# A recurrent GRU and RK4 kernel on one core: GRU work moved on VectorE, ScalarE and GpSimd, and four short matmuls a stage

## The reference

```python
# block 0: GRU, state h
gi = x @ W_ih + b_ih;  gh = h @ W_hh + b_hh
r = sigmoid(i_r + h_r);  z = sigmoid(i_z + h_z)
n = tanh(i_n + r * h_n)
h_new = (1 - z) * n + z * h
# block 1: four Runge-Kutta stages a time step, state q, p; drive = x + GRU's output at this step
i_couple = tanh(q) @ coupling.T
dq = q - q**3 / 3 - p + drive + i_couple + bias
dp = EPSILON * (q + ALPHA - BETA * p)
```

## Time and profile before

| what | us |
|---|---|
| median of 3 runs (lowest, highest) | 3659.93 (3659.13, 3660.63) |
| the profiled execution | 3661.45 |
| its span, first to last instruction | 3659.7 |
| TensorE matmul busy (share) | 3546.2 (97%) |
| TensorE weight load busy | 3220.4 (88%) |
| VectorE busy | 2998.4 (82%) |
| ScalarE busy | 2574.2 (70%) |
| GpSimd busy | 1507.0 (41%) |
| mean granted TensorE clock | 0.989 |

### The profile page before, as it was taken

One profiled execution on the slowest core, in us unless ns is written; L12 is line 12 of the kernel. 1 busy time (PEld: TensorE's weight loads), 2 busy tenths in 40 slices (PEclk: granted clock), 3 DMA queues, 4 the chain that ended last, 5 costly groups with the idle time before them and its releaser, 6 DMA issues.

```text
span 3659.7 us, 298613 instructions
## 1 busy us (share of the span) xinstructions
PE 3546.2 (97%) x115469; PEld 3220.4 (88%) x115469; DVE 2998.4 (82%) x20699; ACT 2574.2 (70%) x22689; POOL 1507.0 (41%) x6169
## 2 busy tenths in 40 slices
PE   8989999999999999999999999999999999999978
PEld 4479999999999999999999999999999999999954
DVE  2078888888888888888888888888888888888876
ACT  3257777777777777777777777777777777777753
POOL 0034444444444444444444444444444444444421
PEclk9999999999999999999999999999999999999978
DMA  3000000000000000000000000000000000000001
GB/s 127 23 25 1 1 1 1 1 1 1 1 1 1 1 1 1 1 1 1 1 1 1 1 1 1 1 1 1 1 1 1 1 1 1 1 1 1 1 2 46
DMA packets 9454, 24.45 MB, mean 7 GB/s; under 512 B 557, under 2 KB 601, under 8 KB 8793
## 3 DMA queue, kind: packets, MB, share of 16 engines
q1 hardware_dynamic: 8832, 19.92, 1.5%
q10 hardware_dynamic: 88, 0.02, 0.0%
HBM read 15.75 MB, written 4.19 MB: 5 GB/s over the span
## 4 chain that ended last, share of the span: by engine, by line
PE 79%; DVE 14%; issue 4%; ACT 3%; DVEq 0%; DMA 0%; ACTq 0%; POOL 0%; POOLq 0%
PE psum L1180 43%; PE psum L1138 29%; PE psum L1108 5%; DVE psum L887 2%; DVE tpart L843 2%; DVE gates L776 2%; ACT tpart L571 1%; PE psum L1283 1%; DVE psum L878 1%; DVE psum L866 1%; DVE fresh L795 1%; DVE narg L787 1%; DVE hs L812 1%; ACT tfull L573 1%; DVE hpart L819 0%
## 5 line engine op out<-in xcount | busy, mean ns | idle before, releaser
L1180 PE MATMUL psum<-tpart,cpl 128*128 128x32 f16 x65536 | 1995.8, 177 | 34.1 <-DVE tpart L843 15.0
L1180 PEld LDWEIGHTS psum<-tpart,cpl 128*128 128x128 f16 x65536 | 1788.7, 96 | 150.9 <-DVE tpart L843 41.5
L1138 PE MATMUL psum<-hpart,whh 128*128 128x32 f16 x49152 | 1622.9, 176 | 28.8 <-DVE hpart L819 24.4
L1138 PEld LDWEIGHTS psum<-hpart,whh 128*128 128x128 f16 x49152 | 1404.1, 96 | 91.5 <-DVE hpart L819 30.4
L843 DVE SCALAR_TENSOR_TENSOR tpart<-tfull,tpart 128x8 f16<-128x8 f32 x4096 | 668.4, 163 | 146.6 <-ACT tfull L573 9.9
L571 ACT ACTIVATE tpart<-psum 128x8 f16<-128x8 f32 x3072 | 544.0, 177 | 245.8 <-DVE psum L887 177.2
L887 DVE TENSOR_REDUCE psum<-psum 128x8 f32<-128x24 f32 x3072 | 585.5, 192 | 133.9 <-PE psum L1180 12.2
L573 ACT ACTIVATE tfull<-psum 128x8 f32<-128x8 f32 x3072 | 529.2, 172 | 0.0
L571 ACT ACTIVATE tpart<-qnext 128x8 f16<-128x8 f32 x1024 | 213.9, 209 | 434.6 <-DVE qnext L887 434.5
L535 ACT ACTIVATE qterm<-psum 128x16 f32<-128x16 f32 x3072 | 400.6, 184 | 111.0 <-DVE psum L866 109.1
L374 POOL TENSOR_TENSOR kept<-rz,hs 128x8 f32<-128x8 f32 x1024 | 209.2, 204 | 466.5 <-ACT rz L500 465.6
(11 more groups left out here) (152 smaller groups left out, 4040.5 us busy)
## 6 DMA issues: line engine op xcount, KB each, us to landing
xrow<-in_x_dram SPq DMA_DIRECT2D x4, 1024.0 KB, 11.3
out_dram<-space SPq DMA_DIRECT2D x16, 256.0 KB, 2.0
wih<-in_L_cond_W_ih_dram SPq DMA_DIRECT2D x3, 1024.0 KB, 9.6
space<-in_L_cond_W_hh_dram SPq DMA_DIRECT2D x1, 3072.0 KB, 18.6
space<-in_L_cond_coupling_dram SPq DMA_DIRECT2D x1, 1024.0 KB, 19.2
xrow<-in_cond_dram SPq DMA_DIRECT2D x1, 1024.0 KB, 4.7
wih<-in_L_cond_Wk_dram SPq DMA_DIRECT2D x1, 1024.0 KB, 5.6
wih<-in_L_cond_Wo_dram SPq DMA_DIRECT2D x1, 1024.0 KB, 8.0
```

What stands on the lines that cost most here:

```text
L1138: mm = pe.matmul(gate_out[x][:, :, :, c * B:(c + 1) * B], whh[:, w, k, n * P:(n + 1) * P], copies_in(hpart[:, k, :, :]), start=(c == 0 and ...
L1180: mm = pe.matmul(stage_out[a][:, :, :, col:col + B], cpl[:, w, k, n * P:(n + 1) * P], copies_in(tpart[:, s % 2, k, :, :]), start=(col == 0 ...
```

## The change

A new tile `omzs` holds omz scaled by s_h; ScalarE fills it (`scaled_omz`, for half 0 in stage 0 behind stage_terms(0), for half 1 in stage 2 behind the first tanh pair), and `weigh` becomes a tensor_tensor of `omzs` and `cand` that waits for it. `split_tanh` becomes a tensor_tensor without the factor 1.0. candidate(1) moves behind the square of stage 2, keep_part(1) on GpSimd behind the sums of stage 2. On VectorE sum_gates(1) moves behind base(2); in stage 3 cubic(3) comes ahead of weigh(1), base(3) ahead of new_high(1), and h_low(1) ahead of the reduction of half a. On TensorE a stage matmul with n = 1 or 3 and k = 3 moves its 8 columns once (`reps`); by the diff these are two matmuls (w = 0, 1) of each half.

```diff
+        omzs = sb("omzs", [P, HALVES, HC])
+        omzs_ready = sem_ab("omzs_ready")
@@ gpsimd, step
-                    if s == 1 and gru <= T:
+                    if s == 2 and gru <= T:
                         keep_part(1, gru)
@@ scalar
+            k_h = act.alloc_register("act_scale_up")
+            act.reg_load(k_h, scale[0:1, 2:3].bitcast(i32))
+            def scaled_omz(x, v):
+
+                act.wait_ge(omz_ready[x], v)
+                act.activation(omzs[:, x, :], omz[:, x, :], ACT.Copy, scale=k_h).then_inc(omzs_ready[x], 1)
@@ scalar, step
                             candidate(0, gru)
+                        if s == 2 and a == 0 and gru <= T:
+                            scaled_omz(1, gru)
                     if s == 2:
                         stage_terms(2)
-                        if gru <= T:
-                            candidate(1, gru)
                     arg, s_next = (in_halves(qnext[:, :]), 0) if s == 3 else (qt, s + 1)
...
                         stage_terms(0)
+                        if gru <= T:
+                            scaled_omz(0, gru)
...
                             sigmoids(1, gru)
+                    if s == 2 and gru <= T:
+                        candidate(1, gru)
                     if s == 2 and gru < T:
                         gate_input(gru + 1)
@@ vector
-                dve.wait_ge(omz_ready[x], v)
+                dve.wait_ge(omzs_ready[x], v)
                 dve.wait_ge(cand_ready[x], v)
-                dve.scalar_tensor_tensor(fresh[:, x, :], omz[:, x, :], s_h, cand[:, x, :],
-                                         ALU.mult, ALU.mult).then_inc(fresh_ready[x], 1)
+                dve.tensor_tensor(fresh[:, x, :], omzs[:, x, :], cand[:, x, :], ALU.mult).then_inc(fresh_ready[x], 1)
...
-                dve.scalar_tensor_tensor(tpart[:, s % 2, a * HK:(a + 1) * HK, 1, :],
-                                         tfull[:, a * HC:(a + 1) * HC].rearrange("p (k b) -> p k b", b=B), 1.0,
-                                         tpart[:, s % 2, a * HK:(a + 1) * HK, 0, :], ALU.mult, ALU.subtract).then_inc(t_parts[s][a], 1)
+                dve.tensor_tensor(tpart[:, s % 2, a * HK:(a + 1) * HK, 1, :],
+                                  tfull[:, a * HC:(a + 1) * HC].rearrange("p (k b) -> p k b", b=B),
+                                  tpart[:, s % 2, a * HK:(a + 1) * HK, 0, :], ALU.subtract).then_inc(t_parts[s][a], 1)
@@ vector, step
                     new_high(0, gru)
                     new_h_full(0, gru)
+                base(2, now)
+                if gated_step:
                     sum_gates(1, gru)
-                base(2, now)
...
+                cubic(3, now)
                 if gated_step:
                     weigh(1, gru)
-                cubic(3, now)
+                base(3, now)
                 if gated_step:
                     new_high(1, gru)
-                base(3, now)
-                if gated_step:
                     new_h_full(1, gru)
-
-                sum_stage(3, 0, now)
                 if gru < T:
                     h_low(1, gru)
+
+                sum_stage(3, 0, now)
                 sum_stage(3, 1, now)
@@ tensor, stage_products
-                            mm = pe.matmul(stage_out[a][:, :, :, col:col + B], cpl[:, w, k, n * P:(n + 1) * P],
-                                           copies_in(tpart[:, s % 2, k, :, :]), start=(col == 0 and k == 0 and w == 0),
+                            reps = 1 if n % HK == HK - 1 and k == K - 1 else COPIES
+                            mm = pe.matmul(stage_out[a][:, 0:reps, :, col:col + B], cpl[:, w, k, n * P:(n + 1) * P],
+                                           copies_in(tpart[:, s % 2, k, :, :])[:, 0:reps, :], start=(col == 0 and k == 0 and w == 0),
```

More of the change, by code:

```diff
@@ L519, in _ @@
                 sigmoids(1, v)
+                scaled_omz(0, v)
+                scaled_omz(1, v)
                 candidate(0, v)
```

## The result

The changed kernel takes 3703.61 us (median of 4 runs, 3702.61 to 3703.99) against 3660.23 for the one before: ratio 1.0119, 95% interval 1.0101 to 1.0136. It is 43.4 us slower, where 53.6 us faster was forecast, and outside the range.

The account below looks back on a forecast made before the run. Stages were taken as bound by a loop of latencies, not TensorE's pace. Gains 0.01 + 0.03 + 0.02 + 0.045 = 0.105 us a step over 510 steps gave 53.6 us, hence 3606 us, range 3574 to 3640.

Parts of the forecast that it names:

- What bounds the kernel: Each stage is a loop of latencies through TensorE and VectorE; TensorE waits 0.07 to 0.34 us in each.
- Eight columns: Stage matmuls ending a half: end about 8 ns sooner, no gain in pace; stages 0 and 1 gain 0.01 us.
- Rival (2): TensorE's stage matmuls: fewer columns also quicken the pace, 0.165 us a step, 3576 us; chance 0.07.
- weigh: VectorE's weigh as tensor_tensor: holds the engine 0.07 us less each time, bounds 0 and 0.15.
- Stage 2: VectorE's new order in stage 2: the split for stage 3 starts 0.02 to 0.06 us sooner; taken as 0.03.
- the exclusion that the prediction names: VectorE tensor_tensor with both inputs in SBUF and GpSimd reading SBUF exclude each other; would cut stage 2's gain to 0.02.
- Stage 3: VectorE's new order from weigh(1) to the reduction of half a: 0.07 to -0.01 us gained, taken as 0.02.
- TensorE's late start of every second stage 0: TensorE's 0.09 us lateness, from gate matmuls waiting for h_low(1), goes: 0.045 us a step gained.
- The gate block of stage 3: Sign on TensorE: with h_low(1) sooner, the gate block lasts 0.77 us and not 0.91.
- (3): VectorE: weigh is no cheaper, delaying sum_gates(1) and stage 3's reduction; 0.035 us a step longer, 3678 us; chance 0.07.
- (1): Only TensorE's stop goes, stages 0 to 2 at lower ends, stage 3 at -0.01; 0.055 a step, 3632 us; chance 0.17.
- (4): The granted clock falls to the half level, half a takes 45 ns longer; 38 us slower, 3698 us; chance 0.03.

Follow-up runs that it names:

- low_back: Changed kernel with h_low(1) moved back between the two reductions of stage 3; 3596.22 us, ratio 0.9824 to the kernel before.
- four_pairs: best_low_behind with four short matmuls at the end of each half instead of two; 3507.07 us, ratio 0.9582 to the kernel before.
- cols_only: The kernel before with the eight-column matmuls alone; 3651.92 us, ratio 0.9977 to the kernel before.
- weigh_stt: low_back with weigh in its old form, scale read from a tensor; 3656.32 us, ratio 0.9987 to the kernel before.
- reorder_only: Changed kernel with all stage matmuls at 32 columns again; 3708.69 us, ratio 1.0130 to the kernel before.
- late_first_low_back: low_back with the late wait written first in weigh, new_high and h_low; 3571.87 us, ratio 0.9760 to the kernel before.
- before_late_first: The kernel before with only the late wait written first in weigh, new_high and h_low; 3569.31 us, ratio 0.9750.
- best_low_behind: late_first_low_back plus the matmuls' wait first in the stage sums (except half a of stage 0) and sum_gates; 3507.67 us, ratio 0.9586 to the kernel before.
- before_waits: The kernel before's order of work with all of best_low_behind's waits and the eight columns; 3528.55 us, ratio 0.9639 to the kernel before.

## Why the prediction was wrong

The step that failed is the sum of stage 3's chain on VectorE from weigh(1) to the reduction. It took two dependent instructions, new_high(1) and h_low(1), for 0.07 us cheaper each than they are, and so saw a gain in moving h_low(1) ahead of the reduction. By terms, forecast and measured:

- *What bounds the kernel*: right. The stages are loops of latencies: in low_back the reduction of stage 3 starts 0.29 sooner and the stage is 0.22 shorter. TensorE's pace wasn't the bound and columns don't set it (four_pairs).
- *Eight columns*: the term holds. 8 ns for a half's end were worked out and 10 measured, and the columns alone are worth 7.5 us (cols_only), where the term's 0.01 a step is 5. Rival (2) is refuted: the starts stay 25 ns apart.
- *weigh*: right within its bounds. Two times 0.07 were put down, two times 0.06 measured (weigh_stt), and its record is 0.167 long and not 0.227. But the 0.11 between the candidate and weigh, in the earlier trace rows, was put down to the read of the scale. It stayed at 0.10 with the scale gone, and fell to 0.04 when the wait was written first.
- *Stage 2*: 0.03 forecast, 0.039 measured. sum_gates(1) behind base(2) did no harm. GpSimd's sums are out of argument(1)'s way, which lasts 0.23 now and not 0.27. keep_part(1) (1536.81 to 1537.01) overlapped its start at 1536.96 and didn't lengthen it, so this trace doesn't bear out the exclusion that the prediction names, for argument's form of instruction; it was not tried by itself.
- *Stage 3*: here it failed, in the terms "base +0.09, new_high(1) +0.09, new_h_full(1) +0.11, h_low(1) +0.19, the reduction +0.11". Measured from weigh's start are 0.11, 0.16, 0.09, 0.26 and 0.11. new_high(1) and h_low(1) each wait for a result that comes last and is the second wait written, 0.07 each above the sum; base brought 0.02, which new_h_full took back, and weigh started 0.34 after the stage's first matmul, 0.02 beyond its upper bound. The reduction came 1.07 after the first matmul, against 0.83 to 0.91 forecast and 0.90 before, and the stage lost 0.125 where 0.02 and 0.045 were to be gained. The rows gave it away: in the earlier trace rows new_h_full ends at 2006.84 and h_low starts at 2006.95, 0.11 later. I took the 0.03 of other pairs.
- *TensorE's late start of every second stage 0*: it was there, and it went, as said. Before, stage 3 lasted 1.705 in one step and 1.797 in the next (means of 200 steps each); in the changed kernel it lasts 1.879 and 1.873. It couldn't be a gain, since the split itself was later than TensorE had been. The gate block of stage 3 lasted 0.83 and not the 0.77 forecast, since h_low(1) starts 0.96 after the stage's first matmul (1.03 before) and not 0.76.
- *Rivals*: the loss was on VectorE in stage 3. (3) had h_low(1) hold the reduction there, but its condition, a weigh that is no cheaper, didn't come, and its price was 18 us. (1) had stage 3 in it with a loss of 0.01 at most. (4) saw the clock fall, but put it down for the whole loop: the falls cover 26 times 3.4 us and cost some 2 us, and with 32 columns throughout (reorder_only) the kernel is as slow with a full clock. Each of the 26 begins in the step behind one of 6.72 to 6.82 us, that is, behind a pause. The changed kernel has 104 steps over 6.7 us and the one before 18. reorder_only has 113 and no fall, cols_only 12 and one, weigh_stt 31 and one; of the kernels faster than these, only low_back has any, 7, and no fall. So the falls of the changed kernel came where its eight columns and its longer steps met; why the clock falls there is open.

## What to carry to other kernels

Before an instruction is put ahead of one on the critical path, take the distance from its producer's end to its start from that very pair in the trace, not from another pair; a dependent chain ahead of the bound instruction costs its idle time besides its busy time (here 0.10 us of waiting ahead of h_low(1)). Where an instruction waits for several semaphores, write the one that comes last first: that alone was worth 90 us here, more than the whole reordering. And try the ordering change again after such a fix, since its worth had shrunk: with the new weigh and the columns it was 64 us at first (low_back), nothing beside three mended waits (late_first_low_back against before_late_first), and without the columns 21 us beside all of them (best_low_behind against before_waits).

## What the runs showed of the hardware

- In these programs an instruction of VectorE with several waits carries the one written first; the others become the sequencer's own. If one of those comes last, the start is 0.104 us after the end of a producer on VectorE, else 0.034; behind ScalarE's candidate, 0.102 against 0.03 to 0.04. For the sums behind the matmuls it is 272 against 203 ns from the matmul's start.
- The recorded span of a matmul with 8 columns is 166 ns, with 32 columns 177 (the changed kernel's groups, shapes kept apart):

```profile
L1195 PE MATMUL psum<-tpart,cpl 128*128 128x32 f16 x57344 | 1892.1, 177 | 123.1 <-DVE tpart L857 115.5
...
L1195 PE MATMUL psum<-tpart,cpl 128*128 128x8 f16 x8192 | 782.9, 166 | 0.0
```

- In the changed kernel, whose stages end with VectorE's split and not with TensorE's pairs, a stretch of 3.4 us at the half level costs some 0.07 us: half a's 20th matmul starts 0.528 after the first and not 0.490, and stages 1 and 2 last 0.03 longer (medians).
